# The last mixing chunk of a one-core transformer kernel, handed over by two engines and two DMA queues instead of one of each

## The reference, cut to what matters

```
h = tok(x, log_dt, log_w_real, w_imag, 512)            # (8, 256, 512)
h = h + attn(layernorm(h), w_q, w_k, w_v, w_o)
h = h + ffn(layernorm(h), select_weight, ..., debias_w)
```

## Time and profile before

| | us |
|---|---|
| median of three runs | 815.27 (814.86 to 816.08) |
| the profiled execution, its own time | 815.9 |
| its span, first to last instruction | 813.8 |
| mixing's last matmul | about 98.2 |
| first projection matmul | 109.71 |

### The profile page before, as it was taken

One profiled execution on the slowest core, in us unless ns is written; L12 is line 12 of the kernel. 1 busy time (PEld: TensorE's weight loads), 2 busy tenths in 40 slices (PEclk: granted clock), 3 DMA queues, 4 the chain that ended last, 5 costly groups with the idle time before them and its releaser, 6 DMA issues.

```text
span 813.8 us, 19725 instructions
## 1 busy us (share of the span) xinstructions
PE 748.4 (92%) x6968; PEld 679.0 (83%) x6968; DVE 571.2 (70%) x1603; ACT 456.3 (56%) x1252; POOL 447.3 (55%) x663
## 2 busy tenths in 40 slices
PE   0377788999999999999999999999999999999996
PEld 0166667899999999999999999999999998988873
DVE  7989868877765655565665566666655777778876
ACT  6734436565567566555575655555756645545432
POOL 1488847655545646444465654444747565565532
PEclk9999999999999999999999999999999999999999
DMA  9023741100010102000001020000100001110104
GB/s 213 0 55 86 173 130 27 39 1 0 0 41 1 53 1 79 0 0 0 0 14 40 10 69 0 0 0 0 30 24 2 1 2 27 26 26 0 27 8 96
DMA packets 32215, 26.47 MB, mean 33 GB/s; under 512 B 23134, under 2 KB 23518, under 8 KB 32166
## 3 DMA queue, kind: packets, MB, share of 16 engines
q1 hardware_dynamic: 32022, 25.77, 12.7%
q10 hardware_dynamic: 144, 0.07, 0.0%
HBM read 17.44 MB, written 8.39 MB: 32 GB/s over the span
## 4 chain that ended last, share of the span: by engine, by line
PE 77%; POOL 7%; DVE 7%; ACT 4%; issue 3%; DMA 1%; DVEq 0%; SPq 0%; POOLq 0%; ACTq 0%
PE bank_quad L1414 17%; PE bank_quad L1416 16%; PE bank_quad L1415 16%; PE bank_pair L1414 4%; PE bank_pair L1416 4%; PE bank_pair L1415 4%; POOL w_lo L480 2%; PE bank_quad L1426 2%; PE bank_quad L1529 2%; PE bank L1607 1%; PE bank_pair L1597 1%; PE bank L1611 1%; PE bank_pair L1607 1%; DVE bank_pair L1043 1%; POOL kq_lo L572 1%
## 5 line engine op out<-in xcount | busy, mean ns | idle before, releaser
L1414 PE MATMUL bank_quad<-xt_hi,w_hi 128*128 (+1 forms) x768 | 216.7, 282 | 1.7 <-POOL w_lo L480 0.8
L1416 PE MATMUL bank_quad<-xt_lo,w_hi 128*128 (+1 forms) x768 | 214.4, 279 | 0.0
L1415 PE MATMUL bank_quad<-xt_hi,w_lo 128*128 (+1 forms) x768 | 214.3, 279 | 0.0
L1130 DVE TENSOR_TENSOR kq<-bank_quad,cst 128x512 f32<-128x512 f32 (+1 forms) x96 | 57.8, 603 | 134.3 <-ACT swap L793 101.2
L567 POOL TENSOR_TENSOR swap<-swap,cst 128x512 f32<-128x512 f32 (+1 forms) x96 | 106.0, 1106 | 81.2 <-ACT swap L793 77.0
L1414 PEld LDWEIGHTS bank_quad<-xt_hi,w_hi 128*128 128x128 f32 x768 | 144.2, 188 | 3.4 <-POOL w_lo L480 1.5
L1416 PEld LDWEIGHTS bank_quad<-xt_lo,w_hi 128*128 128x128 f32 x768 | 144.2, 188 | 0.0
L1415 PEld LDWEIGHTS bank_quad<-xt_hi,w_lo 128*128 128x128 f32 x768 | 143.9, 187 | 0.0
L387 POOL TENSOR_TENSOR spare<-cst 1x1 f32<-1x1 f32 x86 | 17.8, 208 | 200.3 <-DVE rinv L1296 139.7
L838 ACT ACTIVATE sm<-sm,mx 128x128 f32<-128x128 f32 (+1 forms) x256 | 113.6, 445 | 20.6 <-DVE mx L1284 20.6
L792 ACT ACTIVATE swap<-bank_quad 64x512 f32<-64x512 f32 (+1 forms) x96 | 50.3, 524 | 118.0 <-PE bank_quad L1416 115.1
(11 more groups left out here) (332 smaller groups left out, 1867.7 us busy)
## 6 DMA issues: line engine op xcount, KB each, us to landing
mixed<-st SPq DMA_DIRECT2D x32, 128.0 KB, 2.0
x<-mixed SPq DMA_DIRECT2D x32, 128.0 KB, 3.1
out<-x SPq DMA_DIRECT2D x32, 128.0 KB, 2.3
raw<-in_w_qkv SPq DMA_DIRECT2D x8, 384.0 KB, 3.7
raw<-in_w_o SPq DMA_DIRECT2D x10, 256.0 KB, 2.7
norm_mem<-in_w_qkv SPq DMA_DIRECT2D x6, 384.0 KB, 3.7
norm_mem<-in_w_o SPq DMA_DIRECT2D x6, 256.0 KB, 2.8
cim<-in_mix_s SPq DMA_DIRECT2D x4, 256.0 KB, 7.9
```

The lines of the kernel that those rows point to most:

```text
L1130: v.tensor_tensor(view(kq), src, table(cosT), ALU.mult).then_inc(kq_cos, 1)
L1414: mmul(dst, lh, rh, start=start and k == 0, stop=False, skip_group_check=True)
L1415: mmul(dst, ll, rh, start=False, stop=False, skip_group_check=True)
L1416: last = mmul(dst, lh, rl, start=False, stop=stop and k == n - 1, skip_group_check=True)
```

## The change

The last chunk (q = 15, in set 1) is handed over in two halves. DVE copies half 0 from bank 2 and SP stores it; ACT copies half 1 from bank 3 and stores it from its own DMA queue (new semaphores `last_evac` and `last_out`). The first load of tile 1 is split in the same way: SP loads half 0 as soon as its own store and the earlier ones have landed; ACT loads half 1, behind its copy of `cw`, its table load and its Exp. SP waits for `last_out` before it issues the remaining loads.

On DVE the statistics of tile 0 move ahead of the twelve table products, and the copy of half 0 stands behind those products, before `half_apply(0)`. On POOL `early_norm` moves ahead of the wait for `pw_done`, and a new wait for `early_xn` (the end of `half_apply(0)`) stands ahead of all four `split_lo`. PE waits for evacuation 15 instead of 16 and runs `keep_warm(1)` instead of `keep_warm(2)` there.

```diff
@@ SP @@
-            store_mixed(NQ - 1, 1, NQ)
-            for s in range(2):
-                sp.wait_ge(xd_out[s], 16 * 2 * (NQ // 2))
-            load_tokens(1, 0, x_first)
+            sp.wait_ge(last_evac[0], 1)
+            sp.dma_start(mixed_rows[NQ - 1, 0], st[1][:, 0, :, :]).then_inc(xd_out[1], 16)
+            sp.wait_ge(xd_out[0], 16 * 2 * (NQ // 2))
+            sp.wait_ge(xd_out[1], 16 * 2 * (NQ // 2) - 16)
+            load_half(sp, 0, 1, 0, x_first)
+            sp.wait_ge(last_out, 16)
             load_tokens(1, 1, x_second)
@@ POOL @@
-            pool.wait_ge(pw_done, KC)
...
-            split_lo(0)
             early_norm()
-            for n in range(1, KC):
+            pool.wait_ge(early_xn, 1)
+            pool.wait_ge(pw_done, KC)
+            for n in range(KC):
                 split_lo(n)
@@ ACT @@
-            for s in range(2):
-                act.wait_ge(mixed, NQ - 1 + s)
-                act.wait_ge(xd_out[s], (NQ // 2 - 1) * 32)
-                evacuate(NQ - 2 + s, s)
+            act.wait_ge(mixed, NQ - 1)
+            act.wait_ge(xd_out[0], (NQ // 2 - 1) * 32)
+            evacuate(NQ - 2, 0)
+            act.wait_ge(mixed, NQ)
+            act.wait_ge(xd_out[1], (NQ // 2 - 1) * 32)
+            nc.scalar.activation(st[1][:, 1, :, :].rearrange("p m j -> p (m j)"), banks[3][:, 0:4 * 64],
+                                 ACT.Copy).then_inc(last_evac[1], 1)
+            act.wait_ge(last_evac[1], 1)
+            act.dma_start(mixed_rows[NQ - 1, 1], st[1][:, 1, :, :]).then_inc(last_out, 16)
             act.wait_ge(cw_mm, 1)
             nc.scalar.activation(cw[:], banks[7][:, 0:FC], ACT.Copy).then_inc(cw_done, 1)
             nc.scalar.activation(rinv[:, 0:1], cst[:, 0:1], ACT.Exp)
+            act.wait_ge(xd_out[0], 16 * 2 * (NQ // 2))
+            act.wait_ge(last_out, 16)
+            load_half(act, 1, 1, 0, x_first)
@@ DVE @@
+            dve.wait_ge(x_early, 32)
+            norm_stat(lambda t: x[:, t, 0, :], 0)
+            wait_apart(dve, ln_st, 1, 4)
+            v.bn_aggr(norm_set(0)["mv"][:, 0, :], stats[:, 0, :]).then_inc(early_var, 1)
             dve.wait_ge(gate_in, 80)
...
-            dve.wait_ge(x_early, 32)
-            norm_stat(tokens(0), 0)
-            wait_apart(dve, ln_st, 1, 4)
-            v.bn_aggr(norm_set(0)["mv"][:, 0, :], stats[:, 0, :]).then_inc(early_var, 1)
+            dve.wait_ge(mixed, NQ)
+            dve.wait_ge(xd_out[1], (NQ // 2 - 1) * 32)
+            v.tensor_copy(st[1][:, 0, :, :].rearrange("p m j -> p (m j)"), banks[2][:, 0:4 * 64]).then_inc(last_evac[0], 1)
             dve.wait_ge(early_rstd, 1)
             half_apply(0).then_inc(early_xn, 1)
@@ PE @@
-            pe.wait_ge(evac, NQ)
-            keep_warm(2)
+            pe.wait_ge(evac, NQ - 1)
+            keep_warm(1)
```

More of the change, by code:

```diff
@@ L330, in tower @@
             sem("early_lo"), sem("x_early"))
+        last_evac, last_out = [sem(f"last_evacuated{k}") for k in range(2)], sem("last_rows_out")
         pw_done, cw_mm, cw_done = sem("pw_done"), sem("cw_mm"), sem("cw_done")
@@ L359, in tokens_of, with load_half @@
             return slice(first, first + NS)
+        mixed_rows = x_dram.rearrange("(hh q m t) c (a j) -> q hh (t c a) m j", hh=2, q=NQ, t=2, j=64)
+        def load_half(engine, hh, t, b, done):
+            engine.dma_start(x[half_rows(hh), t, b, :], x_dram[tokens_of(hh, t), b, :]).then_inc(done, 16)
         def columns_of(tile, t):
@@ L422, in _ @@
             sp.dma_start(slp[:], slopes.unsqueeze(0).to_broadcast([P, NE])).then_inc(gate_in, 16)
-            rows = x_dram.rearrange("(hh q m t) c (a j) -> q hh (t c a) m j", hh=2, q=NQ, t=2, j=64)
             def store_mixed(q, s, evacuated):
@@ L426, in store_mixed @@
                 for hh in range(2):
-                    sp.dma_start(rows[q, hh], st[s][:, hh, :, :]).then_inc(xd_out[s], 16)
+                    sp.dma_start(mixed_rows[q, hh], st[s][:, hh, :, :]).then_inc(xd_out[s], 16)
             def load_tokens(t, b, done):
                 for hh in range(2):
-                    sp.dma_start(x[half_rows(hh), t, b, :], x_dram[tokens_of(hh, t), b, :]).then_inc(done, 16)
+                    load_half(sp, hh, t, b, done)
             with sp.Fori(0, NQ // 4) as it:
@@ L1074, in _, with norm_stat @@
                         sum_b(s, it * 2 + s)
+            def norm_stat(src, t):
+                v.bn_stats(stats[:, t, :], src(t)).then_inc(ln_st, 1)
+            dve.wait_ge(x_early, 32)
+            norm_stat(lambda t: x[:, t, 0, :], 0)
+            wait_apart(dve, ln_st, 1, 4)
+            v.bn_aggr(norm_set(0)["mv"][:, 0, :], stats[:, 0, :]).then_inc(early_var, 1)
             dve.wait_ge(gate_in, 80)
@@ L1086, in _ @@
                                 dbs[:, k, :].unsqueeze(2).to_broadcast([P, NE, HE]), ALU.mult).then_inc(pw_done, 1)
-            def norm_stat(src, t):
-                v.bn_stats(stats[:, t, :], src(t)).then_inc(ln_st, 1)
             def norm_collect(m):
```

## The result

| | median us (runs) | ratio to before, 95% interval |
|---|---|---|
| before | 815.75 (8) | |
| changed kernel | 817.94 (8) | 1.0023 [1.0012, 1.0034] |

The change costs about 1.9 us by the ratio and 2.2 by the medians. The profiled execution of the changed kernel took 816.78 us with a span of 815.0, against 815.9 and 813.8 before.

A forecast was written before the change was run, and what follows sets the result against it. The prediction took the DMA path (evacuate, store, load) to set the first projection's date, with POOL 0.53 us behind. POOL's +0.45 and the clock's +0.95 gave 815.27 + 1.4 = 816.7 us; own range 816.1 to 817.1, 80% range 814.6 to 818.0.

The forecast's parts named there:

- One date decides and passes through: Start of project_kv(0)'s first matmul, 109.71 us: any shift of it reaches the end of the kernel at full size.
- POOL's list takes the place of the DMA path: Four splits behind early_xn delay POOL's second normalisation from 106.13 to 106.58: +0.45 us, bounds +0.2 and +0.65.
- The apply is short when POOL stands still: DVE's apply of tile 0 takes 0.56 us instead of 2.02 while POOL waits.
- the rival of the slow apply: DVE's apply of tile 0 still takes 2.0 us: 817.2, or 818.1 with the clock's fall; chance 0.04.
- The DMA path gains 0.75: Evacuation, store and load of the last chunk: the load into tile 1 lands at 104.3 instead of 105.06.
- With a landing of 2.2: Last chunk's stores, issued at 98.7, land 2.2 us later (2.0 to 2.8), at 100.9.
- The rival in which the DMA path decides: First projection follows the load into tile 1, 0.75 us earlier: 814.5; chance 0.10.
- The clock falls: PE idles 4.2 us before the second transposes, granted clock falls to 0.5: +0.95 us, bounds +0.45 and +1.4.
- Sum: Whole kernel: 0.45 + 0.95 = +1.4 us, 816.7 from the median; a small loss that will hardly be seen.
- the rival in which the low clock lasts: Transposes, filler and about 2.2 us of projections on PE run at half clock: +2.6, 817.9; chance 0.12.

The follow-up runs named there:

- e8: Kernel before with only the reordering of DVE and POOL, handover as before, keep_warm(2) then keep_warm(7): median 816.53 us, ratio 1.0005.
- e2: Changed kernel without POOL's wait for early_xn ahead of the first split: median 816.29 us, ratio to before 1.0003.
- e1: Changed kernel with keep_warm(8) instead of keep_warm(4) behind the transposes of tile 0: median 816.25 us, ratio to before 1.0003.
- e4: Kernel before without keep_warm(4) behind the transposes of tile 0: median 817.54 us, ratio to before 1.0021.
- e10: Changed kernel profiled again without edit: 20.23 us from the mixing's last matmul to the first large swap, against 19.02 in its first profile.
- e7: Kernel before with only the handover of the last chunk in halves on two engines and two queues: median 816.04 us, ratio 1.0000.
- e5: Changed kernel with POOL's first split ahead of early_norm, no wait for pw_done, keep_warm(7) for keep_warm(4): median 815.52 us, ratio to before 0.9990.
- e9: As e5, but SP issues both stores and both first loads on one queue: median 815.17 us, ratio to before 0.9989.
- e6: As e5, with SP's load of tile 0 of batch 7 moved behind the tile 1 loads of batches 0 to 2: median 815.34 us, ratio 0.9987.
- e3: Changed kernel with keep_warm(8) for keep_warm(4) and without POOL's wait for early_xn: median 816.16 us, ratio to before 1.0000.

## Why the prediction was right in its mechanism and low in its size

- *One date decides and passes through.* Right: in both kernels 201.4 to 201.5 us lie between the `swap` and the later transposes, and 496.7 to 496.8 behind those.
- *POOL's list takes the place of the DMA path.* Right: +0.45 forecast, +0.52 measured, +0.56 with the order alone (e8). Inside it one piece was wrong: `early_norm` gave rstd 1.1 us later against M than I had worked out, since a one-element add in it took 1.34 and not 0.18 (last section), and the apply waited 0.27 for it. The splits started 0.3 later against M for it and were 0.2 quicker than forecast. That the two nearly cancel is luck.
- *The apply is short when POOL stands still.* Right: 0.55, and 2.02 again in e2. The rule of the Trainium skill (SBUF — State Buffer, "Who interferes with whom") that the prediction went by agrees with both numbers, and the rival of the slow apply falls.
- *The DMA path gains 0.75.* Wrong. The step that failed is "With a landing of 2.2": it took a row measured with one queue for two stores at once, which took 2.7 and 2.9, so that ACT issued its load at M + 3.44 and not M + 3.0. Then the load took 3.3 and not 3.1. The gain was 0.13. It cost the forecast nothing, because POOL hid it. The rival in which the DMA path decides would have been mis-sized by it.
- *The clock falls.* Right in place and in cause, shown by e1 (taken away) and e4 (made alone). The term of the sum that was mis-sized is this one: +0.95, with bounds 0.45 and 1.4. It measured 1.06, 2.27 and 0.90 in three profiles and 1.6 to 1.8 in the medians (changed against e1, e4 against before). I had counted one low stretch as the rule and two as a rival at 0.12. After 4.4 and 5.0 us of idleness two came in two of four profiles (e4, e10), and then the filler and over 2 us of projections run at half speed. That second stretch is the price that the forecast left to the rival.
- *Sum.* +1.4 forecast, +1.9 to +2.2 measured. The interval, 1.0012 to 1.0034, lies wholly above 1, so the loss can be told from no change, where I had written that it would hardly be seen. 817.94 is above the forecast's own range (816.1 to 817.1) and only 0.06 inside the 80% range. About 0.5 of the distance from 816.7 is no part of the change: the median of before was 815.75 in this comparison and 815.27 in the three runs that I started from. So it is chance, too, that 817.94 meets the 817.9 of the rival in which the low clock lasts: that one wanted +2.6.

Open: whether the fall near 138 us, seen in the changed kernel's first profile, e2, e4 and e7 and not in the others, costs anything in other executions. In the profiles read here it doesn't: from the `swap` to the later transposes it is 201.4 to 201.6 us with it and 201.1 to 201.6 without.

## What to carry to other kernels

Before a wait is shortened, look at the list of the engine that is next: here POOL was 0.53 us behind, and the same change lengthened its list. Fillers have to last until shortly before the work that must run at full clock: idle times of 0.7 to 1.7 us at this place saw no fall in any profile, 4.4 us and more saw one in every profile, and 3.0 us (e2) lies between. When transposes move forward, count PE's idle time behind them again, for here it cost three times what POOL did. Two queues for the two halves of one transfer were no gain here; splitting the evacuation and keeping the transfers in order on one queue, the needed ones first, was the fastest of the orders tried by the dates, though the times don't separate it.

## What the runs showed of the hardware that I had not expected

- A one-element add on POOL took 1.34 us at 96.26 instead of 0.18, and 1.34 again in e8. Beside it DVE ran its twelve table products, most of which read two operands from SBUF, and both times the add ended 0.05 us behind the last of them. The Trainium skill (SBUF — State Buffer, "Who interferes with whom") has it that a DVE instruction with two SBUF inputs contends with a GpSimd instruction that reads SBUF. The trace fits, but the products alone don't explain it: in e5 they ran beside the same add too, and it took 0.18 (0.22 in e9). There POOL came to it straight from a split, and not out of 1.75 us of idleness. Why that matters stays open. The timelines of DVE and POOL in e5:

```profile
95.28 0.25 DVE L1105 TENSOR_TENSOR vtab<-fw 128x64 f32<-128x64 f32 x1
...
95.43 0.18 POOL L393 TENSOR_TENSOR spare<-cst 1x1 f32<-1x1 f32 x1
```

- Two stores of 128 KB from two queues took 2.7 and 2.9 us each, from one queue 2.2 and 2.3, and the later one landed at nearly the same date. The Trainium skill (DMA: Bandwidth & Descriptors, "Issuing engines are not separate DMA queues") says that a second issuing engine saves only issue time. Here not even that was left for the load that counts, which went out at M + 3.36 with two queues and M + 3.37 with one, and with two queues that load took 0.53 us longer.
- From the first projection to the first large `swap` at full clock it takes either 5.93 us (before, e1, e6, e9) or 5.73 (e3, e5, e7, e8), with the same instructions. The 0.2 is no single wait: the 48 matmuls of the projection start 0.118 us apart in the former and 0.113 in the latter (means up to 114 us), at a granted clock of 1.00 in both. In e5, e7 and e8 it is 0.2 longer than in before from the `swap` to the transposes 200 us on, so nothing is left of it. I have no cause for it.
